# Causal corner of the transposed scores: set to zero by GpSimd after the exponential, in place of a mask product on PE before it

## The chip, the cores and the metric

One core of one Trainium2 chip runs the whole program. The metric is the device time in microseconds of one execution, and the time of a kernel is the median of its runs. The engines are PE (TensorE, matrix products into PSUM), DVE (VectorE), ACT (ScalarE), POOL (GpSimd) and SP (SyncE, which here only issues DMAs). Each engine works through its own instructions in order, and semaphores tie the engines together.

## The reference, cut to what matters

The program computes two transformer layers over 2 batches of 1024 tokens with 128 channels. The change touches the attention of layer 0:

```
Q, K, V = split_heads(h @ WQ.T), split_heads(h @ WK.T), split_heads(h @ WV.T)   # 16 heads of 8
scores  = einsum('bhqd,bhkd->bhqk', Q, K) / sqrt(8)
scores  = where(tril(ones(S, S)), scores, -1e9)
m       = max(scores, axis=-1)
e       = exp(scores - m)
out     = einsum('bhqk,bhkd->bhqd', e / sum(e), V)
```

After it come layer 0's mixture of 64 experts, a four-layer recurrent block (RWKV) and a mixture of 8 experts; none of them is edited. Attention wants an exact zero in e wherever the key comes after the query.

## The kernel before, in words

`build` runs `stage_front` (loads, layer norm, projections), `stage_core` (attention, then the 64 experts), `stage_rwkv_in`, `stage_rwkv` and `stage_last`. The 32 (batch, head) pairs are worked off in 8 groups of 4 heads (`NG`, `HG`).

In a group the scores are computed twice. **Fills** (`fills`, L693) compute them with queries on the partitions, up to 512 columns to a piece, into one of three PSUM banks; DVE takes the maximum of each piece (L1098), and PE may write a bank again only when the piece three items earlier has been reduced (`await_bank`). A group has 38 such pieces. The maxima are negated and split in three bf16 parts on DVE (`negate`, L1102), turned by PE (`turn_neg`, L748), copied by DVE to `neg_t` (L1128) and carried by three DMAs (L592) into three extra rows of `qa`. **Units** (`scores`, L713) then compute the transposed scores with keys on the partitions, the maxima already subtracted by those extra rows. A group has 24 units (`UNITS`: query chunk c of 512, key tile j of 128, pair p of heads): 8 with c=0 and 16 with c=1. A unit is two products of up to 512 columns, one per head. ACT takes the exponential of both (L945) into one of four slots of `pt`. Two units, p=0 and p=1, make one step q; after them `outputs` (L733) multiplies the four heads' `pt` with the values `va_g` into the accumulator bank: eight f32 products (L743).

A unit whose key tile lies on the diagonal (j >= 4c) gets, behind each of its two products, a third operand added into the first 128 columns of the bank: identity times `mask_kq` (L729), a 128x128 bf16 tile with -1e30 where the key comes after the query. There are 16 such units to a group, 4 in each step q, so 32 mask products a group and 256 in all. The fills have mask products of their own (L709, `mask_qk`), which are not edited.

PE's order is written out in `group` (L835): for each unit u the fills of `FRONT[u]`, perhaps a `turn_neg`, `scores(g, u)`, the fills of `BACK[u]`, and at odd u >= 3 `outputs` of step (u-3)/2, that is of the two units before last. The last step of a group is output after unit 1 of the next group; in the last group it follows at once. `SPREAD` deals the fills of group g+1 over the units of group g; group 0 does the rest of its own as well. The last group has no fills; beside its units run the output projection, layer norm, logits and routing of the first token chunks (`beside`). A unit waits for the exponential of the unit two before it (`prob_done`), ACT waits before it overwrites a slot of `pt` until the slot's `outputs` are done (`pv_done`).

POOL makes `ident`, `mask_qk`, `mask_kq` and zeroed `va_g` at the start (L191 to L206), and in attention it only copies the values of each group into one of the two `va_g` (`keep_v`, L679), when the outputs of the group two before have ended. SP's queue for each group: load of the group three ahead, then `pack` (results out of `acc`), then `neg_rows`.

Of the kernel before, what the change touches and what calls it, by code (L numbers as in the profile page):

```python
# [6 lines left out]
ALU = mybir.AluOpType  # L7
ACT = mybir.ActivationFunctionType
F32 = mybir.dt.float32
BF16 = mybir.dt.bfloat16  # L10
AX_X = mybir.AxisListType.X

P = 128
# [9 lines left out]
NG = B * H // HG  # L23
NEG = -1e30
# [36 lines left out]
def chunk(c, n=CH):  # L61
    return slice(c * n, (c + 1) * n)
# [54 lines left out]
def stage_front(nc, G, A):  # L117

    mem = G.mem
    with ExitStack() as ctx:  # L120
# [17 lines left out]
        pool_zero, const_done = mem.sem("pool_zero"), mem.sem("const_done")  # L138
# [15 lines left out]
        with nc.Block() as block:  # L154
# [34 lines left out]
            @block.gpsimd  # L189
            def _(pool):  # L190
                pool.memset(G.ident[:, :], 0.0).then_inc(pool_zero, 1)  # L191
                pool.memset(G.mask_qk[:, :], 0.0).then_inc(pool_zero, 1)
                pool.memset(G.mask_kq[:, :], 0.0).then_inc(pool_zero, 1)
                pool.wait_ge(pool_zero, 3)
                pool.affine_select(out=G.ident[:, :], in_=G.ident[:, :], compare_op=ALU.not_equal, fill=1.0, base=0,
                                   pattern=[[-1, P]], channel_multiplier=1).then_inc(const_done, 1)

                pool.affine_select(out=G.mask_qk[:, :], in_=G.mask_qk[:, :], compare_op=ALU.is_ge, fill=NEG, base=0,
                                   pattern=[[-1, P]], channel_multiplier=1).then_inc(const_done, 1)
                pool.affine_select(out=G.mask_kq[:, :], in_=G.mask_kq[:, :], compare_op=ALU.is_ge, fill=NEG, base=0,  # L200
                                   pattern=[[1, P]], channel_multiplier=-1).then_inc(const_done, 1)
                for k in range(2):
                    pool.memset(G.va_g[k][:, :, :, :], 0.0).then_inc(pool_zero, 1)
                pool.wait_ge(pool_zero, 5)
                for k in range(2):
                    pool.memset(G.va_g[k][:, :, :, 1:32:4], 1.0).then_inc(G.v_pad, 1)  # L206

# [47 lines left out]
            def _(dve):  # L255
# [44 lines left out]

                dve.memset(G.mean[:, :], 1.0 / P).then_inc(centre_done, 1)
                dve.memset(G.eps[:, :], 1e-5).then_inc(centre_done, 1)
                dve.wait_ge(const_done, 3)
                dve.tensor_scalar(G.centre[:, :], G.ident[:, :], -1.0 / P, None, ALU.add).then_inc(centre_done, 1)
                dve.tensor_copy(G.identb[:, :], G.ident[:, :]).then_inc(centre_done, 1)
                dve.memset(ones_row[:, :, :], 1.0).then_inc(centre_done, 1)
# [26 lines left out]
            def _(pe):  # L333
                def turn_x(c):
                    pe.wait_ge(x_in[c], 16)
                    if c == 3:
                        pe.wait_ge(x_kept, 2)
                    for t in range(4):
                        mm = pe.transpose(x_bank[c][:, chunk(t, P)], x_tok[:, 4 * c + t, :], G.ident[:, :])
                    mm.then_inc(x_turned, 1)  # L340
# [28 lines left out]
                        pe.wait_ge(x_kept, c)  # L369
                    ln_centre(pe, G, c, G.x[:, chunk(c)])  # L370

                pe.wait_ge(const_done, 3)
                turn_x(0)
                pe.wait_ge(centre_done, 4)
                centre(0)
# [3 lines left out]
                for i in range(3):  # L379
                    mm = pe.transpose(G.bank[4][:, chunk(i, P)], w_nat[:, i, :], G.ident[:, :])  # L380
# [63 lines left out]
def stage_core(nc, G, A):  # L444
# [4 lines left out]
    mem = G.mem  # L449
# [4 lines left out]
             for n in [min(HG, CH // min(CH, (i + 1) * P - k0))] for h in range(0, HG, n)]  # L454
    NF = len(FILLS)
    HALF = sum(i < 4 for _, _, i, _, _, _ in FILLS)

    UNITS = [(c, j, p) for c in range(2) for j in range(4 * c + 4) for p in range(2)]
    NU = len(UNITS)
    NQ = NU // 2  # L460
# [23 lines left out]
    LAST = NG - 1  # L484
# [9 lines left out]
    with ExitStack() as ctx:  # L494
# [3 lines left out]
        pt = m.sb("pt", [P, 4, 2, CH])  # L498
# [24 lines left out]
        hid = m.sb("moe_hid", [P, NC, CH])  # L523
        factor = [t[:, k, :, :].rearrange("p h t -> p (h t)").bitcast(F32) for t in (qa, ka) for k in range(2)]

        v_in = mem.sem("v_in")
        piece_psum, piece_max = mem.sem("piece_psum"), mem.sem("piece_max")
        max_step = mem.sem("max_step")
        neg_turned, neg_kept = mem.sem("neg_turned"), mem.sem("neg_kept")
# [1 line left out]
        score_psum, prob_done, pv_done = mem.sem("score_psum"), mem.sem("prob_done"), mem.sem("pv_done")  # L531
# [52 lines left out]
        with nc.Block() as block:  # L584
# [92 lines left out]
            @block.gpsimd  # L677
            def _(pool):
                def keep_v(k, g):  # L679
                    pool.tensor_copy(va_g[k][:, :, :, 0:32:4],  # L680
                                     G.va[:, bass.ds(g, 1), :, :].rearrange("p o t (h d) -> p (o t) h d", h=HG))\
                        .then_inc(v_in, 1)

                pool.wait_ge(G.v_pad, 2)
                for g in range(2):
                    keep_v(g, g)
                for g in range(2, NG):
                    pool.wait_ge(pv_done, NQ * (g - 1))
                    keep_v(g % 2, g)

            @block.tensor
            def _(pe):
# [20 lines left out]
                def scores(g, u):  # L713
                    c, j, p = UNITS[u]
                    q0 = max(CH * c, P * j)
                    n = CH * (c + 1) - q0
                    if u == 0:
                        pe.wait_ge(neg_in, 48 * (g + 2) if g else 48)
                    if NU * g + u == TURN_AT[0]:
                        pe.wait_ge(neg_in, 96)  # L720
                    if NU * g + u >= 2:
                        pe.wait_ge(prob_done, NU * g + u - 1)
                    for k in range(2):
                        out = score_bank[u % 2][:, k, :]
                        diagonal = j >= 4 * c
                        mm = pe.matmul(out[:, 0:n], ka[0:ROWS + 3, g % RING, 2 * p + k, chunk(j, P)],  # L726
                                       qa[0:ROWS + 3, g % RING, 2 * p + k, q0:q0 + n], start=True, stop=True)
                        if diagonal:
                            mm = pe.matmul(out[:, 0:P], G.identb[:, :], G.mask_kq[:, :], start=False, stop=True,  # L729
                                           skip_group_check=True)  # L730
                    mm.then_inc(score_psum, 1)

                def outputs(g, k, q):  # L733
                    c, j, _ = UNITS[2 * q]
                    q0 = max(CH * c, P * j)
                    n = CH * (c + 1) - q0
                    pe.wait_ge(prob_done, NU * g + 2 * q + 2)
                    if q == 0:
                        pe.wait_ge(v_in, g + 1)
                    if j == 0 and (not isinstance(g, int) or 2 * g + c):  # L740
                        pe.wait_ge(acc_kept, 2 * g + c)
                    for h in range(HG):
                        mm = pe.matmul(acc_bank[32 * h:32 * h + 32, q0 - CH * c:CH], va_g[k][:, j, h, :],  # L743
                                       pt[:, 2 * (q % 2) + h // 2, h % 2, 0:n], start=(j == 0),
                                       stop=(j >= 4 * c), skip_group_check=True)
                    mm.then_inc(pv_done, 1)
# [1389 lines left out]
def build(nc, A, out):  # L2136
    G = Global()
    with ExitStack() as ctx:
        mem = G.mem = Memory(nc, ctx)
# [3 lines left out]
        G.ident = mem.sb("ident", [P, P])  # L2143
        G.identb = mem.sb("identb", [P, P], BF16)
        G.mask_qk = mem.sb("mask_qk", [P, P], BF16)
        G.mask_kq = mem.sb("mask_kq", [P, P], BF16)
        G.mean = mem.sb("mean", [P, P])
        G.centre = mem.sb("centre", [P, P])
        G.eps = mem.sb("eps", [P, 1])
# [64 lines left out]
```

## Time and profile before

| | us |
|---|---|
| median of 3 runs | 1193.19 |
| runs | 1193.03 to 1208.87 |
| profiled execution | 1198.58 |
| its span, first to last instruction | 1196.7 |

| engine | busy in the span |
|---|---|
| PE | 1063.7 (89%) |
| DVE | 767.2 (64%) |
| ACT | 578.4 (48%) |
| POOL | 12.1 (1%) |

The profile is of one execution. The span covers first to last instruction; 1.9 us of the execution lie around it. PE's busy time has modelled ends, so a matmul's own duration is longer than the distance to the next one where they follow closely; for the cost of one in a row of them the distance between starts is read. PEclk is the granted clock of TensorE as a share of 2.4 GHz; it has two levels, 0.5 (1.2 GHz) and 1.

### The profile page before, as it was taken

How to read it: one execution, taken by the hardware profiler on the slowest of the kernel's cores; microseconds unless marked ns; L12 is line 12 of the kernel's file. 1: busy time of each engine (PE TensorE's matmuls, PEld its weight loads, DVE VectorE, ACT ScalarE, POOL GpSimd, SP SyncE). 2: the span in 40 equal slices, each digit the busy share in tenths (PEclk: the TensorE clock that was granted, in tenths of full speed). 3: DMA queues.
4: the chain of work that ended last, by engine and by line, in shares of the span. 5: the costliest groups of instructions: out<-in, count | busy, mean ns of one | idle time of the engine just before them, and what ended most of it. 6: DMA issues, size and time to landing. Idle time of an engine off the chain costs nothing. (4 is left out here: it accounts for less than half of the span.)

```text
span 1196.7 us, 13244 instructions
## 1 busy us (share of the span) xinstructions
PE 1063.7 (89%) x4046; PEld 463.8 (39%) x4046; DVE 767.2 (64%) x1327; ACT 578.4 (48%) x904; POOL 12.1 (1%) x26
## 2 busy tenths in 40 slices
PE   6788999999779999999999996498898898898698
PEld 3333444444334444444444432133333333343332
DVE  5867788887556555555555554676776776776465
ACT  5224566667644222222222224666666666767332
POOL 1000000000000000000000000000000000000000
PEclk9768999999989999999999999799899899899899
DMA  3721022200141545555555520000000000000100
GB/s 116 207 60 41 11 50 50 51 24 10 30 90 40 123 91 117 125 122 113 114 108 125 125 45 28 0 21 9 1 20 9 0 20 0 0 0 1 27 9 26
DMA packets 49975, 64.62 MB, mean 54 GB/s; under 512 B 17570, under 2 KB 41232, under 8 KB 45328
## 3 DMA queue, kind: packets, MB, share of 16 engines
q1 hardware_dynamic: 49100, 63.28, 22.5%
q10 hardware_dynamic: 832, 0.79, 0.2%
q8 instruction: 24, 0.39, 0.1%
q14 instruction: 19, 0.16, 0.0%
HBM read 55.87 MB, written 5.77 MB: 52 GB/s over the span
## 5 line engine op out<-in xcount | busy, mean ns | idle before, releaser
L1098 DVE TENSOR_REDUCE part_max<-psum 128x1 f32<-128x512 f32 (+3 forms) x304 | 188.1, 659 | 54.0 <-PE psum L709 31.6
L945 ACT ACTIVATE pt<-psum 128x1024 f32<-128x1024 f32 (+1 forms) x192 | 151.1, 813 | 141.1 <-PE psum L729 104.0
L1257 DVE TENSOR_TENSOR moe_gu<-moe_silu,psum 128x512 f32<-128x512 f32 x132 | 90.8, 688 | 152.0 <-PE psum L861 147.2
L1082 ACT ACTIVATE moe_silu<-psum 128x512 f32<-128x512 f32 x112 | 66.9, 597 | 200.0 <-PE psum L856 200.0
L856 PE MATMUL psum<-h,moe_wt 128*128 128x512 f32 x264 | 135.6, 595 | 1.6 <-ACT moe_silu L1050 1.6
L861 PE MATMUL psum<-h,moe_wt 128*128 128x512 f32 x264 | 135.2, 593 | 0.5 <-DVE moe_gu L1257 0.5
L866 PE MATMUL psum<-moe_hid,moe_wt 128*128 128x512 f32 x264 | 135.0, 593 | 0.7 <-DVE moe_hid L1265 0.7
L705 PE MATMUL psum<-ka,qa 72*128 72x512 bf16 (+3 forms) x384 | 121.8, 360 | 5.5 <-DMA ka<-rows_k 3.5
L726 PE MATMUL psum<-qa,ka 75*128 75x512 bf16 (+3 forms) x384 | 107.8, 344 | 7.1 <-DMA qa<-neg_t 6.8
L1265 DVE TENSOR_TENSOR moe_hid<-moe_gu,qa 128x512 f32<-128x512 f32 x120 | 83.1, 693 | 13.6 <-DVE moe_gu L1257 5.7
L1542 PE MATMUL psum<-kf,wt_c 128*128 128x512 f32 x128 | 67.8, 656 | 24.2 <-ACT kf L1671 24.2
L743 PE MATMUL psum<-pt,va_g 128*32 128x512 f32 (+3 forms) x768 | 86.6, 525 | 0.2 <-ACT pt L945 0.2
L861 PEld LDWEIGHTS psum<-h,moe_wt 128*128 128x128 f32 x264 | 49.9, 190 | 65.0 <-issue 61.5
L856 PEld LDWEIGHTS psum<-h,moe_wt 128*128 128x128 f32 x264 | 49.9, 191 | 64.3 <-issue 64.3
L1532 PE MATMUL psum<-mix_c,wt_c 128*128 128x512 f32 x128 | 62.9, 604 | 12.1 <-ACT relu L1668 12.1
L705 PEld LDWEIGHTS psum<-ka,qa 72*128 72x128 bf16 x384 | 39.3, 104 | 82.6 <-DVE part_max L1098 55.2
L866 PEld LDWEIGHTS psum<-moe_hid,moe_wt 128*128 128x128 f32 x264 | 48.0, 190 | 51.3 <-issue 49.5
L92 ACT ACTIVATE ln_sq<-psum 128x512 f32<-128x512 f32 x48 | 28.3, 602 | 57.3 <-PE psum L75 57.3
L83 PE MATMUL psum<-ln_sq,mean 128*128 128x512 f32 x96 | 50.1, 629 | 4.8 <-ACT ln_sq L92 4.7
L729 PE MATMUL psum<-mask_kq,identb 128*128 128x128 bf16 x256 | 53.5, 228 | 0.0
L726 PEld LDWEIGHTS psum<-qa,ka 75*128 75x128 bf16 x384 | 38.5, 103 | 38.3 <-DMA qa<-neg_t 8.4
L709 PE MATMUL psum<-mask_qk,identb 128*128 128x128 bf16 x256 | 53.3, 235 | 0.0
(251 smaller groups left out, 1394.7 us busy)
## 6 DMA issues: line engine op xcount, KB each, us to landing
qa<-comb_rows SPq DMA_DIRECT2D x56, 512.0 KB, 6.2
qa<-rows_q SPq DMA_DIRECT2D x21, 192.0 KB
ka<-rows_k SPq DMA_DIRECT2D x21, 192.0 KB
o_den<-acc SPq DMA_DIRECT2D x32, 64.0 KB, 2.2
moe_raw<-in_L_ffn_eg_w SPq DMA_DIRECT2D x32, 64.0 KB, 5.6
moe_raw<-in_L_ffn_eu_w SPq DMA_DIRECT2D x32, 64.0 KB, 5.4
moe_raw<-in_L_ffn_ed_w SPq DMA_DIRECT2D x32, 64.0 KB, 5.1
qa<-comb_rows SPq DMA_DIRECT2D x16, 128.0 KB, 3.1
```

Of the source, the lines that this page charges most:

```text
L705: mm = pe.matmul(bank[:, nk * h:nk * (h + 1)], qa[0:ROWS, g % RING, h0 + h, chunk(i, P)], ka[0:ROWS, g % RING, h0 + h, k0:k0 + nk], start= ...
L726: mm = pe.matmul(out[:, 0:n], ka[0:ROWS + 3, g % RING, 2 * p + k, chunk(j, P)], qa[0:ROWS + 3, g % RING, 2 * p + k, q0:q0 + n], start=True ...
L743: mm = pe.matmul(acc_bank[32 * h:32 * h + 32, q0 - CH * c:CH], va_g[k][:, j, h, :], pt[:, 2 * (q % 2) + h // 2, h % 2, 0:n], start=(j == 0 ...
L856: pe.matmul(g_bank[:, :], weights[:, 0, :], G.h[:, chunk(c)], start=True, stop=True).then_inc(g_psum, 1)
L861: pe.matmul(u_bank[:, :], weights[:, 1, :], G.h[:, chunk(c)], start=True, stop=True).then_inc(u_psum, 1)
L866: pe.matmul(y_bank[c][:, :], weights[:, 2, :], hid[:, at, :], start=first, stop=last, skip_group_check=True).then_inc(y_psum, 1)
L945: act.activation(pt[:, u % 4, :, 0:n], score_bank[u % 2][:, :, 0:n], ACT.Exp, scale=SCALE)\
L1082: act.activation(sg[:, c % 2, :], g_bank[:, :], ACT.Silu).then_inc(silu_done, 1)
L1098: dve.tensor_reduce(part_max[:, h0:h0 + heads, slot], bank_of("fill", f)[:, 0:heads * nk].rearrange("p (h n) -> p h n", h=heads), AX_X, AL ...
L1257: dve.tensor_tensor(gu[:, at % 2, :], sg[:, at % 2, :], u_bank[:, :], ALU.mult).then_inc(gu_done, 1)
L1265: dve.tensor_tensor(hid[:, at, :], gu[:, at % 2, :], tile[:, chunk(c)], ALU.mult).then_inc(hid_done, 1)
L1542: mm = pe.matmul(G.bank[4 + q][:, :], wt_c[:, WCV + j, :], kf[:, j, q, :], start=(j == 0), stop=(j == 3))
```

## The change

The 256 mask products and `mask_kq` go. POOL instead overwrites, after the exponential, the first 128 columns of both heads of a diagonal unit's slot of `pt` with zero where the key comes after the query: one `affine_select` of 128x256 f32 per diagonal unit, 16 a group, 128 in all. A diagonal step's `outputs` additionally waits for the two selects of its units (`masked`). `keep_v` for group g+1 now follows the eighth select of group g in POOL's queue.

```diff
-                pool.memset(G.mask_kq[:, :], 0.0).then_inc(pool_zero, 1)
-                pool.wait_ge(pool_zero, 3)
+                pool.wait_ge(pool_zero, 2)
...
-                pool.affine_select(out=G.mask_kq[:, :], in_=G.mask_kq[:, :], compare_op=ALU.is_ge, fill=NEG, base=0,
-                                   pattern=[[1, P]], channel_multiplier=-1).then_inc(const_done, 1)
...
-                dve.wait_ge(const_done, 3)
+                dve.wait_ge(const_done, 2)
...
-                pe.wait_ge(const_done, 3)
+                pe.wait_ge(const_done, 2)
...
+                def mask(g, u):
+
+                    pool.wait_ge(prob_done, NU * g + u + 1)
+                    pool.affine_select(out=pt[:, u % 4, :, 0:P], in_=pt[:, u % 4, :, 0:P], compare_op=ALU.is_ge, fill=0.0,
+                                       base=0, pattern=[[0, 2], [1, P]], channel_multiplier=-1).then_inc(masked, 1)
+
                 pool.wait_ge(G.v_pad, 2)
                 for g in range(2):
                     keep_v(g, g)
-                for g in range(2, NG):
-                    pool.wait_ge(pv_done, NQ * (g - 1))
-                    keep_v(g % 2, g)
+                for g in range(NG):
+                    for u in range(NU):
+                        c, j, _ = UNITS[u]
+                        if j >= 4 * c:
+                            mask(g, u)
+                        if u == 7 and 1 <= g < LAST:
+                            pool.wait_ge(pv_done, NQ * g)
+                            keep_v((g + 1) % 2, g + 1)
...
                     for k in range(2):
                         out = score_bank[u % 2][:, k, :]
-                        diagonal = j >= 4 * c
                         mm = pe.matmul(out[:, 0:n], ka[0:ROWS + 3, g % RING, 2 * p + k, chunk(j, P)],
                                        qa[0:ROWS + 3, g % RING, 2 * p + k, q0:q0 + n], start=True, stop=True)
-                        if diagonal:
-                            mm = pe.matmul(out[:, 0:P], G.identb[:, :], G.mask_kq[:, :], start=False, stop=True,
-                                           skip_group_check=True)
                     mm.then_inc(score_psum, 1)
...
                     pe.wait_ge(prob_done, NU * g + 2 * q + 2)
+                    if j >= 4 * c:
+                        pe.wait_ge(masked, 16 * g + 8 * c + 2 * (j - 4 * c) + 2)
```

## Rows read from the trace of the kernel before

**Rows 1.** The page: PE over the span, the clock in 40 slices, the mask products.

```profile
PE 1063.7 (89%) x4046; PEld 463.8 (39%) x4046; DVE 767.2 (64%) x1327; ACT 578.4 (48%) x904; POOL 12.1 (1%) x26
PEclk9768999999989999999999999799899899899899
L729 PE MATMUL psum<-mask_kq,identb 128*128 128x128 bf16 x256 | 53.5, 228 | 0.0
```

**Rows 2.** Windows: stretch, length, busy PE, PEld, DVE, ACT, POOL, clock, DMA.

```profile
115.00:120.00 5.00, 5.00 (x26) 2.20 (x25) 2.67 (x4) 2.70 (x4) 0.64 (x1) 0.51 0.62 133
182.24:212.47 30.23, 30.23 (x259) 13.96 (x258) 24.82 (x45) 19.42 (x27) 0.66 (x1) 1.00 0.22 50
212.47:214.72 2.25, 2.25 (x27) 1.48 (x26) 2.06 (x4) 2.25 (x5) 0.66 (x1) 1.00 0.75 160
217.16:219.41 2.25, 2.25 (x27) 1.35 (x26) 1.92 (x4) 0.87 (x2) 0.00 (x0) 1.00 0.40 73
240.20:242.70 2.50, 2.50 (x23) 1.10 (x21) 2.34 (x4) 1.11 (x2) 0.00 (x0) 1.00 0.35 99
```

**Rows 3.** Timeline of units 0 and 1 of group 4: start, duration, instruction.

```profile
211.59 1.94 ACT L945 ACTIVATE pt<-psum 128x1024 f32<-128x1024 f32 x2 [1.39 <-PE psum L729]
211.61 0.38 PE L726 MATMUL psum<-qa,ka 75*128 75x512 bf16 x1
211.82 0.22 PE L729 MATMUL psum<-mask_kq,identb 128*128 128x128 bf16 x1
211.88 0.38 PE L726 MATMUL psum<-qa,ka 75*128 75x512 bf16 x1
212.99 0.66 POOL L680 COPY va_g<-va 128x256 f32<-128x256 f32 x1 [29.57 <-PE psum L743]
214.72 1.07 PE L743 MATMUL psum<-pt,va_g 128*32 128x512 f32 x8
```

**Rows 4.** Timeline: a later step of the same group, and DVE's run of reduces.

```profile
209.06 5.55 DVE L1098 TENSOR_REDUCE part_max<-psum 128x1 f32<-128x512 f32 x8 [0.46 <-PE psum L709]
216.49 1.16 ACT L945 ACTIVATE pt<-psum 128x512 f32<-128x512 f32 x2 [1.07 <-PE psum L729]
219.41 0.64 PE L743 MATMUL psum<-pt,va_g 128*32 128x256 f32 x8
```

**Rows 5.** Timeline of group 0 at the low clock, its first and tenth mask, DVE behind.

```profile
55.63 0.31 PE L729 MATMUL psum<-mask_kq,identb 128*128 128x128 bf16 x1
66.67 0.31 PE L729 MATMUL psum<-mask_kq,identb 128*128 128x128 bf16 x1
66.78 0.53 PE L705 MATMUL psum<-ka,qa 72*128 72x384 bf16 x1
67.45 5.34 DVE L1098 TENSOR_REDUCE part_max<-psum 128x1 f32<-128x384 f32 x9 [0.47 <-PE psum L709]
```

**Rows 6.** Timeline: DMAs of the negated maxima, the wait at the end of group 0.

```profile
109.25 1.82 SPq L592 DMA_DIRECT2D qa<-neg_t  x3
114.53 0.39 PE L726 MATMUL psum<-qa,ka 75*128 75x512 bf16 x1 [2.77 <-DMA qa<-neg_t]
205.83 1.82 SPq L592 DMA_DIRECT2D qa<-neg_t  x3
```

**Rows 7.** Groups by line, POOL's selects.

```profile
L195 POOL TENSOR_SCALAR_AFFINE_SELECT ident<-ident 128x128 f32<-128x128 f32 x1 | 0.3, 294 | 0.2 <-POOL mask_kq L193 0.2
L1941 POOL TENSOR_SCALAR_AFFINE_SELECT expand<-expand 24x512 bf16<-24x512 bf16 x3 | 2.2, 746 | 0.4
```

**Rows 8.** Timeline: DVE beside a POOL memset at the start, and a larger one alone.

```profile
2.21 1.83 POOL L203 MEMSET va_g<- 128x1024 f32 x2
2.29 1.83 DVE L304 TENSOR_SCALAR centre<-ident 128x128 f32<-128x128 f32 x1 [1.27 <-POOL mask_kq L200]
308.32 0.49 DVE L1164 TENSOR_SCALAR h<-h,mod 128x512 f32<-128x512 f32 x1
```

**Rows 9.** Timeline: the end of the last group.

```profile
347.63 0.38 ACT L945 ACTIVATE pt<-psum 128x256 f32<-128x256 f32 x1
348.06 0.43 PE L743 MATMUL psum<-pt,va_g 128*32 128x128 f32 x8 [0.22 <-ACT pt L945]
```

More of the change, by code:

```diff
@@ L199, in _ @@
                                    pattern=[[-1, P]], channel_multiplier=1).then_inc(const_done, 1)
-                pool.affine_select(out=G.mask_kq[:, :], in_=G.mask_kq[:, :], compare_op=ALU.is_ge, fill=NEG, base=0,
-                                   pattern=[[1, P]], channel_multiplier=-1).then_inc(const_done, 1)
                 for k in range(2):
                     pool.memset(G.va_g[k][:, :, :, :], 0.0).then_inc(pool_zero, 1)
-                pool.wait_ge(pool_zero, 5)
+                pool.wait_ge(pool_zero, 4)
                 for k in range(2):
@@ L524, in stage_core @@
         factor = [t[:, k, :, :].rearrange("p h t -> p (h t)").bitcast(F32) for t in (qa, ka) for k in range(2)]
-        v_in = mem.sem("v_in")
+        v_in, masked = mem.sem("v_in"), mem.sem("masked")
         piece_psum, piece_max = mem.sem("piece_psum"), mem.sem("piece_max")
@@ L2145, in build @@
         G.mask_qk = mem.sb("mask_qk", [P, P], BF16)
-        G.mask_kq = mem.sb("mask_kq", [P, P], BF16)
         G.mean = mem.sb("mean", [P, P])
```

## The prediction

> **What bounds the kernel now.** I read the page first: PE is busy 89% of the span, and the clock row is 8 or 9 nearly throughout [rows 1]. That is an average, so the windows come next. One group of attention in its steady state is 30.23 us long, PE is busy for all of it, DVE for 24.82, ACT for 19.42 and POOL for 0.66, at the full clock (2.4 GHz) [rows 2]. Groups 2 to 5 all repeat this length: POOL's copy of the values, once a group, sits idle 29.57 us and works 0.66 [rows 3]. PE's busy time is modelled, so I checked it by distances in the timeline: a product of 512 columns takes 0.21 us to the next start, a mask product of 128 columns 0.06 [rows 3]. Products, outputs and masks follow one another like this through the whole group with no hole. So in this stage PE is the bound, and what leaves PE's stream shortens the group, until DVE (24.8) or something new takes over. Everything after attention (from about 350 us on) is untouched, and simply starts earlier.
>
> **Price of what goes.** There are 256 mask products [rows 1], 32 to a group. The mean of 228 ns on the page is latency, not cost. At the full clock one costs the 0.06 us from its start to the next product; I use 0.058, from the runs of such masks in the trace, of which [rows 3] has one. So 32 x 0.058 = 1.85 us per group at most. At the low clock (1.2 GHz) it is 66.78 - 66.67 = 0.11 us [rows 5]. Their weight loads run beside other products and are worth nothing.
>
> *Group 0.* Ten masks lie between 55.63 and 66.67, at the low clock, ahead of the point where DVE falls behind and runs nine reduces without a gap from 67.45 [rows 5]. They are on the path: 10 x 0.107 = 1.1 us. The rest of the group I cost at nothing, for two covers: up to about 108 us its units carry a whole group's fills in a dozen units, and DVE reduces without gaps; and from 109.25 to 114.53 the group's end waits for the negated maxima, PE idle for 2.77 us [rows 6]. PE only arrives there 0.5 us sooner and waits longer.
>
> *Group 1.* Eight masks at the low clock (the clock is 0.51 from 115 to 120 [rows 2]) and 24 at the full one: 0.86 + 1.39 = 2.2 us. I take off 0.1: 2.1.
>
> *Groups 2 to 6.* 1.85 each, less two things. First, DVE. In the steps from 240.20 to 242.70 (last of a group) and 212.47 to 214.72 (first of a group) DVE is busy 2.34 of 2.50 and 2.06 of 2.25 [rows 2]. With four masks (0.23) out of each, PE would want 2.27 and 2.02, 4.29 together, against 4.40 of DVE. The others have room (1.92 against 2.02 from 217.16 [rows 2]). Three banks smooth some of it; I take 0.25 us a group as lost to DVE, between 0.1 (the bare difference) and 0.6. Second, the new wait, below: 0.1. That leaves 1.5 a group; group 6 has a tail without fills, where PE already waits for ACT, so 1.2 there. 4 x 1.5 + 1.2 = 7.2 us.
>
> *Group 7.* PE waits here for DVE and ACT in the layer norm and routing chains, and some half of the 32 masks lie on the path: 16 x 0.06 = 1.0 us. Against it, the last step's outputs start 0.05 us after the last exponential (348.01 to 348.06) [rows 9]; now a select stands between, +0.65, and the packing of the last results hangs on it. Net +0.4 us, between -1.5 and +2.2.
>
> **Price of what comes.** A select of 128x256 f32 is not in the trace. Below, one of 128x128 f32 took 0.294; above, one of 512 elements a partition took 0.746 [rows 7]. On the line between them 256 elements make 0.294 + 128/384 x 0.452 = 0.44, and I take that, since the cost is nearest to a matter of elements a partition; a POOL copy of the same 128x256 took 0.66 [rows 3]. POOL's work is then 16 x 0.44 + 0.66 = 7.7 us of a group's 28.7: no bound. Around the select lie two releases. POOL's copy starts 0.09 us after the outputs' modelled end (212.90 to 212.99), and I allow 0.1 for the way back to PE: 0.65 us from the end of an exponential to the outputs, between 0.5 and 1.0.
>
> What is the room? The outputs of a step come two units after its own. The tightest step is the first of a group: exponentials end at 211.59 + 1.94 = 213.53, outputs start at 214.72, room 1.19 us [rows 3]. Without the eight masks of units 0 to 3 PE gets there 0.46 sooner, and the exponentials only 0.12 sooner: room 0.85. 0.65 fits, barely, and with 1.0 it costs 0.15; hence 0.1. The other diagonal steps have 1.7 us or more (217.65 to 219.41 [rows 4]), about 1.3 after the change. Behind a late `outputs` on PE stand the next fills and units, and on ACT the slot of `pt`; both are late by the same 0.1 and no more. The extra wait instruction on PE is free: the first step of a group has three waits and no larger gap than the others.
>
> DMAs: the maxima of the next group are issued from 205.83 to 207.65 [rows 6] and land some 1.9 later, near 209.6, and are wanted near 211: after the change still over 1 us early. `keep_v` now stands behind the eighth select, half a group ahead of its use: free. At the start a memset and a select of 128x128 go, 0.4 us of POOL, but PE's first transposes wait for the token DMA: nothing.
>
> **Lock on the SBUF port.** At the start a DVE operation of 128x128 took 1.83 us beside a POOL memset, where a 128x512 one in the last group took 0.49 [rows 8]. So the two engines can hold each other up. DVE's reduces from PSUM show none of it: eight in 5.55 us, 0.69 each, with POOL's copy of 0.66 among them [rows 3, 4]. The Trainium skill ("SBUF — State Buffer", section "SBUF: two separate sides") says that DVE and GpSimd share a port pair under an exclusive lock, which a DVE instruction takes when it has two SBUF inputs or runs in a 2-port mode. By that rule the reduces stay free, but the five small operations of `negate`, which fall among diagonal units, and the selects would stall each other.
>
> **Sum.** 1.1 + 2.1 + 7.2 + 0.4 = 10.8 us off the profiled 1198.58: 1187.8. The profiled execution is 5.4 above the median of the runs, 1193.19; against the median it is 1182.4, and I say 1182.
>
> **Rivals.**
> - *DVE takes over* (14%). For it: DVE is at 82% of a group and at 94% in its tightest step [rows 2]. If each handshake costs and a group gives 0.9 instead of 1.5, the gain is 7.5: about 1186. Against it: DVE still waits for PE in most steps.
> - *The lock* (12%). Up to three selects of 0.44 fall into the chain of negated maxima, whose transpose PE reaches 0.7 us after DVE is done. Delays of 0.9 to 1.3 would stop PE for some 0.4 a group; with seven groups, 2.8 us less: 1185. It decides where the delay passes 0.5 us. For it: [rows 8]; against: DVE's operations there are 0.18 us each.
> - *POOL becomes the bound, slower than before* (6%). In each half of a group eight selects must fit into about 8 us, from the first exponential's end to the fourth outputs. Beyond 1.0 us a select every tenth costs 0.8 us per half: 16 x (d - 1.0) a group. The gain is gone at d = 1.1; at d = 1.4 it is 8 x 6.4 = 51 us lost against 11 gained, 1233. Against it: no select took over 0.75 [rows 7].
> - *The clock* (8%). After idle stretches it stays low for some 10 us, as behind 114.53 [rows 2, 6]. PE idles a little longer there now and reaches the next units at other moments; half the clock for 5 us more or less is 2.5 us of PE. 1178 or 1186.
> - *Nothing is gained* (4%): the removed products were filler under a wait that the trace doesn't show. 1193.
>
> **Chances and range.** The forecast, 1179 to 1185, has 56%. If all 256 masks were earned, (238 x 0.058 + 18 x 0.107) = 15.7, it would be 1177.5; with clock luck 1175. The other side reaches to no gain and a little noise of the median: 1195. A measurement of this kernel tells about 2% (24 us) from no change. Faster by more is out of the masks' reach, 3% for the clock; slower by more needs POOL as bound, 5%; within, 92%.
>
> **What would show it.** Group periods near 28.7 at POOL's copies; no L729; selects near 0.44, and POOL's busy near 70 us; outputs' waits for POOL only in a group's first step and at the very end; DVE's busy per group unchanged at 24.8. Wrong would be: selects over 1 us, PE idle before L743 in many steps, or a group still of 30 us.

## The result and the profile after

| | before | after |
|---|---|---|
| median of 6 runs each, same chip (us) | 1199.82 | 1184.85 |
| lowest to highest | 1193.03 to 1208.87 | 1181.74 to 1187.65 |
| profiled execution / its span | 1198.58 / 1196.7 | 1187.65 / 1185.9 |

The ratio is 0.9878, with a 95% interval of 0.9829 to 0.9926: 1.2% faster, less than the 2% that the prediction named as tellable, but the interval leaves out 1. Two later repetitions of the changed kernel gave 0.992 [0.989, 0.9951] and 0.9863 [0.9817, 0.991]; a repetition of the kernel before gave 1.0018 [0.998, 1.0056]. Predicted was 1182 in a range of 1175 to 1195.

The page of the changed kernel, answering to [rows 1]: busy time of each engine, the clock in 40 slices, then the groups of the outputs and of the selects (busy, mean ns | idle before, and its releaser).

```profile
PE 1054.5 (89%) x3790; PEld 449.3 (38%) x3790; DVE 765.4 (65%) x1327; ACT 577.6 (49%) x904; POOL 63.7 (5%) x152
PEclk9769999999789999999999999799999999999799
L749 PE MATMUL psum<-pt,va_g 128*32 128x512 f32 (+3 forms) x768 | 86.3, 523 | 0.9 <-POOL pt L684 0.8
L684 POOL TENSOR_SCALAR_AFFINE_SELECT pt<-pt 128x256 f32<-128x256 f32 x128 | 52.4, 410 | 234.0 <-ACT pt L951 233.2
```

The 256 mask products are gone from PE's count (4046 to 3790). The selects took 52.4 us of POOL, and in the whole program PE waited 0.8 us for them. POOL itself mostly waits for ACT (233.2 us): it is nowhere near a bound.

Where did the time go? I laid the executions side by side by one landmark, ACT's first exponential of each group, and for the end PE's first product of the experts. The second pair is a later repetition of both kernels. "Gain" is before less after, in us; the spans' difference is the sum.

| stretch | predicted | before | after | gain | gain, second pair |
|---|---|---|---|---|---|
| start to group 0 | 0 | 56.52 | 60.73 | -4.2 | +2.9 |
| group 0 | 1.1 | 58.77 | 54.78 | +4.0 | +0.5 |
| group 1 | 2.1 | 35.84 | 29.67 | +6.2 | +5.9 |
| groups 2 to 5 | 6.0 | 120.91 | 114.96 | +6.0 | +5.9 |
| group 6 | 1.2 | 30.24 | 29.16 | +1.1 | +1.1 |
| group 7 | 0.4 | 46.14 | 48.01 | -1.9 | -2.2 |
| the rest | 0 | 848.28 | 848.59 | -0.3 | +0.3 |
| sum | 10.8 | 1196.7 | 1185.9 | 10.8 | 14.4 |

The sum of the first pair equals the predicted 10.8, and that is partly luck: groups 2 to 6 came as predicted, group 1 gave three times its term, the last group lost, and the start and group 0 vary from execution to execution.

A steady group answers to the second row of [rows 2]. The windows (stretch, length, busy PE, PEld, DVE, ACT, POOL, clock) of group 4 after the change:

```profile
202.82:231.48 28.66, 28.63 (x226) 11.81 (x225) 24.16 (x44) 19.34 (x26) 7.07 (x17) 1.00 0.23 54
```

28.66 us in place of 30.23, 33 fewer products counted, PE still busy all of it, POOL at 7.07 (predicted 7.7). PE is still the bound of this stage.

Because single executions differ by more than 10 us, here are all timed executions of this study, where each kernel's time stands against the mean granted clock of its core. At each of the ten clock levels that both have, the changed kernel is below the kernel before; five of them (means of the executions):

| mean granted clock | before: mean us (executions) | changed: mean us (executions) |
|---|---|---|
| 0.941 | 1208.5 (1) | 1190.7 (2) |
| 0.947 | 1198.2 (5) | 1187.1 (5) |
| 0.948 | 1194.9 (1) | 1186.2 (5) |
| 0.951 | 1194.1 (8) | 1182.6 (3) |
| 0.954 | 1192.0 (5) | 1181.5 (1) |

Ten of the 91 executions of the kernel before were in a slower state, over 1.5% above its fastest, and are left out of what follows. One straight line, common to all kernels, has 7.9 us for every 0.01 of clock, and the changed kernel lies 12.9 +- 1.0 us below the kernel before (81 and 24 executions). Their medians differ by 12.3, 1198.99 to 1186.68. So most of the spread of a kernel's times goes with the clock, and the gain is real and a little larger than the predicted 10.8.

### The profile page after: what moved, and what is told of

Same layout as the page of the kernel before. It is cut to its first block and busy times, and to the rows that moved or that the text cites. A ratio compares the mean times of both kernels' runs of the same rounds, so it can differ in the third digit from the quotient of the medians.

```text
span 1185.9 us, 12921 instructions
## 1 busy us (share of the span) xinstructions
PE 1054.5 (89%) x3790; PEld 449.3 (38%) x3790; DVE 765.4 (65%) x1327; ACT 577.6 (49%) x904; POOL 63.7 (5%) x152
## 5 line engine op out<-in xcount | busy, mean ns | idle before, releaser
L1104 DVE TENSOR_REDUCE part_max<-psum 128x1 f32<-128x512 f32 (+3 forms) x304 | 185.0, 658 | 39.7 <-PE psum L717 25.3
L733 PE MATMUL psum<-qa,ka 75*128 75x512 bf16 (+3 forms) x384 | 99.0, 343 | 5.2 <-DMA qa<-neg_t 4.9
L1548 PE MATMUL psum<-kf,wt_c 128*128 128x512 f32 x128 | 71.3, 686 | 24.2 <-ACT kf L1677 24.2
L684 POOL TENSOR_SCALAR_AFFINE_SELECT pt<-pt 128x256 f32<-128x256 f32 x128 | 52.4, 410 | 234.0 <-ACT pt L951 233.2
L1518 PE MATMUL psum<-hp,wt_a 128*128 128x512 f32 x96 | 50.0, 603 | 3.1 <-DVE hp L1755 3.1
```

The costliest lines, as they stand in the source:

```text
L1104: dve.tensor_reduce(part_max[:, h0:h0 + heads, slot], bank_of("fill", f)[:, 0:heads * nk].rearrange("p (h n) -> p h n", h=heads), AX_X, AL ...
L1548: mm = pe.matmul(G.bank[4 + q][:, :], wt_c[:, WCV + j, :], kf[:, j, q, :], start=(j == 0), stop=(j == 3))
```

## Experiments

All times are medians, and ratios are to the kernel before on the same chip.

### The two kernels again: r_before, r_after, r_after_again

No edit; they give the second traces.

> The kernel before, unchanged, for a second trace. Question: which parts of the gap between the two first traces belong to the change, and which to the execution. In the first traces the changed kernel's first exponential came 4.2 us later (60.73 against 56.52), its group 0 was 4.0 us shorter (54.8 against 58.8) and its group 1 was 6.2 us shorter (29.7 against 35.8), since no stretch at 1.2 GHz stood behind the wait for the maxima at the end of group 0. Theory 'luck': front, group 0 and group 1 of this kernel differ from its own first trace by several us, with the place of the slow-clock stretches, while groups 2 to 5 are again 30.23 us each. Theory 'structure': it repeats 56.5, 58.8 and 35.8 within 0.5 us.

> The changed kernel, unchanged. Both theories: groups 2 to 5 again 28.66 us (one or two 0.3 longer). 'Structure': group 1 again 29.7 us, since PE idles 0.84 us before it; 'luck': group 1 somewhere between 28.7 and 35. Total against the kernel before: 0.986 to 0.992 (the steady groups alone give 8 us, 0.7%).

> The changed kernel once more: last group 48.0, groups 2 to 5 28.66 to 29.0, group 1 29.66 us. Group 0 between 54.8 and 60.3 us, by the length of the slow-clock stretch (55 and 57 us so far).

Measured: r_before 1200.81 us; r_after 1187.05 us; r_after_again 1186.32 us. Their steady groups are 30.23 and 28.66 to within 0.01, as in the first traces, but for one (group 3 of r_after, 29.04, of which more below). Their group 0 is 57.36 before and 56.82 and 57.58 after (first traces 58.77 and 54.78): the same program differs there by 2.8 us between executions, so the 1.1 us predicted for this group can't be confirmed or refuted. The third trace of the changed kernel brought the largest surprise, a last group of 45.58 us instead of 48.01; it is taken up below.

### What do the selects cost? e_nomask

```diff
-                        if j >= 4 * c:
-                            mask(g, u)
...
-                    if j >= 4 * c:
-                        pe.wait_ge(masked, 16 * g + 8 * c + 2 * (j - 4 * c) + 2)
```

> The changed kernel without the 128 selects and without PE's waits for them; the upper corner of the diagonal tiles is left unmasked. It measures what GpSimd's part costs. My theory (hidden in the steady groups, 0.63 us at the last step and some port contention in the last group): groups 2 to 5 stay at 28.66 us, the last group (first exponential to the first expert product) is 1 to 2 us shorter than the 48.0 of the changed kernel, total 1 to 2 us faster. Rival (the select's latency or the port lock costs in every group): groups 2 to 5 fall to 28.4 us or below, since 32 mask products at 0.058 us are 1.85 us and only 1.57 were seen.

Measured: 1185.01 us, ratio 0.9891 [0.9858, 0.9924]. Group 4 of this kernel, same columns:

```profile
201.00:229.53 28.53, 28.53 (x226) 11.80 (x225) 24.26 (x45) 19.35 (x27) 0.65 (x1) 1.00 0.20 49
```

28.53 against 28.66: sixteen selects and the waits for them cost PE 0.13 us of a group. That is the price of the handshake in the steady state; predicted was 0.1. The profile shows no wait of PE for a select in these groups, so at which instructions the 0.13 arises stays open.

### Is DVE next? e_dve_half

The reduces read half of their columns; everything else is the changed kernel.

```diff
-    bank_of("fill", f)[:, 0:heads * nk].rearrange("p (h n) -> p h n", h=heads),
+    bank_of("fill", f)[:, 0:heads * nk].rearrange("p (h n) -> p h n", h=heads)[:, :, 0:nk // 2],
```

> The changed kernel, with DVE's maxima taken over the first half of each piece's columns alone (wrong maxima, DVE's work in attention about halved). The steady groups lost 30.23 - 28.66 = 1.57 us where 32 mask products at 0.058 are 1.85. Theory (the missing 0.28 us is DVE's, 0.13 of it seen without selects): groups 2 to 5 at 28.4 to 28.55 us. Rival (it is PE's own: the products cost less than 0.058 in place, or the selects' waits take it): 28.66 as before. Group 0, where DVE reduces without gaps for 12 us, gets 1 to 3 us shorter in either case.

Measured: 1185.75 us (2 runs), ratio 0.9883 [0.9802, 0.9965]. Its group 4:

```profile
201.82:230.24 28.42, 28.42 (x227) 11.82 (x225) 16.21 (x45) 19.35 (x26) 7.08 (x17) 1.00 0.25 60
```

With DVE at 16.21 instead of 24.5 a group takes 28.42. So DVE's work holds PE up by 0.24 us a group in the changed kernel, where 0.25 was predicted. If nothing else held PE up on either side, 30.23 - 28.42 = 1.81 us is what the 32 masks were worth, against 1.85 from the distances in the trace. The 0.24 here and the 0.13 of e_nomask can't be added: together they are 0.37, and a group came out only 0.28 above 30.23 - 1.85. Taking away either the selects or half of DVE's work removes a part of the same wait, and no run removes both.

### How much slower may the selects be? e_sel2 and e_sel3

The select is done two or three times in a row, each waiting for the one before (here three):

```diff
-                    pool.affine_select(...).then_inc(masked, 1)
+                    for i in range(3):
+                        ins = pool.affine_select(...)
+                        if i < 2:
+                            ins.then_inc(again, 1)
+                            again_n[0] += 1
+                            pool.wait_ge(again, again_n[0])
+                    ins.then_inc(masked, 1)
```

> The changed kernel with each select run twice. In the run with three, 34 selects stood in a row at 0.44 us from one to the next, so a unit cost 1.31 us and a diagonal step 2.62, and the steps' distance was 2.62: periods of 32.06. Theory (a step takes the longer of PE's own 2.0 to 2.9 us and twice the select): with 2 x 0.44 = 0.88 a unit, 1.76 a step, POOL stays below PE in every step; only the first step of a group, with 0.85 us of room, waits: periods 28.8 to 29.3 us. Rival (the latency of each select adds to every step): 8 x 0.44 = 3.5 us more, 32 us again.

> The changed kernel, with each select run three times in a row, each waiting for the one before (about 3 x 0.41 + 2 x 0.25 = 1.7 us per unit in place of 0.41). It looks for the point from which POOL decides. My rule in the prediction was 16 x (d - 1.0) us a group beyond d = 1.0: 16 x 0.7 = 11 us a group, periods near 40 us and the kernel some 80 us slower than the changed one. Rival (the room behind a step absorbs it: the steps' own period of 2.0 to 2.9 us holds two selects only up to about 1.1): the same sign, but counted as 2 x d against the step, 8 steps x (3.4 - 2.4) = 8 us a group, periods near 36.5 us.

Measured: e_sel2 1191.32 us, 0.993 [0.9887, 0.9973]; e_sel3 1208.51 us, 1.0072 [1.0033, 1.0111]. Windows of a steady group of each (e_sel2, then e_sel3):

```profile
176.70:205.80 29.10, 28.73 (x227) 11.79 (x226) 24.73 (x45) 19.34 (x26) 13.44 (x34) 1.00 0.23 53
```

```profile
184.39:216.45 32.06, 28.99 (x230) 12.08 (x225) 24.85 (x45) 19.42 (x27) 19.62 (x50) 1.00 0.20 47
```

The expectation for e_sel3 took each repeated select to be dearer than it is. In the trace they follow one another at 0.44 us (a run of them, below, with 19 in 8.25 us), so three make 1.31 us a unit, not 1.7, and both numbers expected for the group were too long.

```profile
184.04 8.25 POOL L685 TENSOR_SCALAR_AFFINE_SELECT pt<-pt 128x256 f32<-128x256 f32 x19
```

What happens is simple all the same. A diagonal step has two units, so 2 x 1.31 = 2.62 us of POOL, where PE alone needs 2.0 to 2.9; the outputs in this stretch come 2.6 to 2.7 us apart, and the group grows by 3.4 us. At 0.87 us a unit (e_sel2) only 0.4 is lost. The point from which POOL bounds a diagonal half thus lies between 0.87 and 1.31 us a unit; my rule 16 x (d - 1.0) gives 5.0 at 1.31 where 3.4 was measured. At three times the POOL work the kernel is 0.7% slower than before, at twice it is still 0.7% faster. For e_sel2 the expected period of 28.8 to 29.3 us came true (29.06).

### Masks back on PE in the last group, or in its last step: e_last_pe, e_last_pe_again, e_step_pe

```diff
-                        if j >= 4 * c:
+                        if j >= 4 * c and g < LAST:
                             mask(g, u)
...
+                        if g == LAST and j >= 4 * c:
+                            mm = pe.matmul(out[:, 0:P], G.identb[:, :], G.mask_kq[:, :], start=False, stop=True,
+                                           skip_group_check=True)
...
-                    if j >= 4 * c:
+                    if j >= 4 * c and g < LAST:
                         pe.wait_ge(masked, 16 * g + 8 * c + 2 * (j - 4 * c) + 2)
```

`mask_kq` is made again, as before the change. e_step_pe does the same for the last diagonal step only.

> The changed kernel, with the last group alone masked by PE as before (32 mask products at that place, no selects and no waits there). Theory (in the last group the products were mostly hidden and the select's latency is on the path at the end): last group 46 to 47.5 us against 48.0, total 0.5 to 2 us faster than the changed kernel, so the best version so far. Rival (the 1.9 us that the last group lost were a slow-clock stretch at another place): last group as long as in the changed kernel or longer by up to 1 us for the products.

> The changed kernel with the last group masked by PE, once more, beside the changed kernel. By the traces it should be 2.3 us (0.2%) faster, since the last group takes 45.7 us in place of 48.0. In its first run it was 0.5 us faster in the median, with an interval of 0.3%. Expected: 1 to 3 us under the changed kernel in the median, last group 45.5 to 46 us; group 0 anywhere from 54.8 to 60.3 us, with the length of the slow-clock stretch.

> The changed kernel, with the very last step (group 7, j = 7) alone masked by PE: 4 mask products back, 2 selects and their wait gone. The last group took 48.0 us with selects, 46.2 with no mask at all and 45.7 with products. Theory 'end': PE's wait of 0.77 us for the last select is on the path and is all that this step costs: 47.2 us; the remaining 1.3 us come from selects in front of DVE's work on layer norm and routing and from the earlier waits. Rival 'all of it': 46.2 us or less. Total 0.5 to 1 us under the changed kernel, within its noise.

Measured: e_last_pe 1186.59 us, 0.9912 [0.9878, 0.9946]; e_last_pe_again 1188.06 us, 0.9892 [0.9846, 0.9939]; e_step_pe 1187.44 us, 0.9881 [0.9821, 0.9941].

First the end itself. The timeline of the changed kernel's last units: the last exponential, the last select, the last outputs, the first product of the experts.

```profile
335.95 0.38 ACT L951 ACTIVATE pt<-psum 128x256 f32<-128x256 f32 x1
336.40 0.41 POOL L684 TENSOR_SCALAR_AFFINE_SELECT pt<-pt 128x256 f32<-128x256 f32 x1 [0.34 <-ACT pt L951]
336.96 0.42 PE L749 MATMUL psum<-pt,va_g 128*32 128x128 f32 x8 [0.77 <-POOL pt L684]
337.31 0.30 PEld L862 LDWEIGHTS psum<-h,moe_wt 128*128 128x128 f32 x2 [0.20 <-issue]
```

The exponential ends at 336.33, the outputs start at 336.96: 0.63 us with a select between, where [rows 9] had 0.05. The predicted chain was 0.65. With the masks back on PE (e_last_pe_again) it is 0.05 again:

```profile
331.49 0.38 ACT L957 ACTIVATE pt<-psum 128x256 f32<-128x256 f32 x1
331.92 0.43 PE L755 MATMUL psum<-pt,va_g 128*32 128x128 f32 x8 [0.42 <-ACT pt L957]
```

So 0.58 us at the end of the last group are the select's, shown. The rest of its 1.9 us are not. At first I put all of it down to the selects, because the last group was 48.01, 48.01 and 47.63 with selects (after, r_after, e_step_pe), and 45.69 and 45.05 without (e_last_pe twice), 46.16 in e_nomask. Then r_after_again, a repetition of the changed kernel, took 45.58 with all sixteen selects. The windows of the same stretch, 22 us after the group's first exponential, tell the two apart; the last three columns are clock, DMA share and GB/s. First the first trace of the changed kernel, then r_after_again:

```profile
311.30:321.30 10.00, 9.54 (x33) 3.61 (x32) 6.61 (x22) 5.23 (x8) 0.00 (x0) 0.53 0.13 33
```

```profile
311.82:321.82 10.00, 9.10 (x44) 3.44 (x44) 7.93 (x34) 6.73 (x10) 0.00 (x0) 0.83 0.12 32
```

The profile has 33 products of PE in one and 44 in the other. At 0.53 it spent almost the whole window at 1.2 GHz, at 0.83 a third of it. Both executions slowed down after the same stretch in which PE waited for other engines (the 6 us before it had PE busy 4.52); they differ in how soon the full clock came back. So the 2.4 us between these two executions of one kernel are a matter of the clock, not of selects in PE's way. They are in part paid back behind the group: "the rest" takes 851.67 us in r_after_again, against 848.63 in r_after. Over the first 20 products of PE behind the group it has the clock at 0.72 and takes 12.16 us, where the first trace of the changed kernel has 0.84 and takes 10.68:

```profile
335.40:347.56 12.16, 8.93 (x20) 3.78 (x17) 7.79 (x37) 4.69 (x7) 0.00 (x0) 0.72 0.41 107
337.31:347.99 10.68, 7.44 (x20) 3.31 (x17) 7.40 (x36) 4.69 (x7) 0.00 (x0) 0.84 0.58 121
```

Neither expectation of the other two runs came true. e_last_pe_again was to be 1 to 3 us faster than the changed kernel: its trace has the shorter last group, but its median is 1.7 us above that of r_after_again. e_step_pe was to have a last group of 47.2 us, or 46.2 by the rival: its last outputs follow their exponential by 0.05 us again, but the group took 47.63, with the long slow stretch in it. Of the version with the masks kept on PE no gain was measured: 1187.16 us, against 1186.68 of the changed kernel (18 and 24 executions; 1 or 2 us would not be seen in these medians).

r_after_again also shows what the edit is worth in this group at a like clock (0.88 up to the last exponential, in the kernel before 0.89). Its last exponential starts 44.22 us after the group's first one (289.82), in the kernel before 347.63 - 302.28 = 45.35 [rows 9]; its last outputs are again 0.63 behind that exponential's end:

```profile
334.04 0.38 ACT L951 ACTIVATE pt<-psum 128x256 f32<-128x256 f32 x1
335.05 0.42 PE L749 MATMUL psum<-pt,va_g 128*32 128x128 f32 x8 [0.98 <-POOL pt L684]
```

That is 1.13 us less without the masks. Against two other traces with masks on PE and a clock of 0.89 it is 0.80 (r_before, 45.02) and 0.68 (e_last_pe, 44.90). So 0.7 to 1.1 us are won by the masks that went, where 1.0 was forecast, and 0.58 given back by the select.

Whether the selects make the long slow stretch likelier stays open. Four of the five traces with single selects and full reduces have it (after, r_after, e_step_pe and e_after_pad, 47.6 to 48.0 us). Of the six whose last group has none, only e_before_pad has it (from 20 to 32 us into the group; 46.01 us, because it was spared a later stretch near 43 us that the first trace of the kernel before has). So it is not tied to them alone. But the traces do not acquit the selects: from the last group's first exponential to the end of the program the same five take 896.5 to 897.3 us, r_after_again the most, and the same six 893.5 to 895.3. Beside it stands that the medians show no gain for the version with the masks kept on PE.

### What made group 1 so much shorter? e_before_pad and e_after_pad

Group 1 gained 6 us, and the masks can't be worth more than 2.2. The windows of its first 8 us, kernel before, then changed kernel:

```profile
115.29:123.29 8.00, 8.00 (x37) 2.80 (x35) 4.06 (x6) 4.25 (x5) 0.64 (x1) 0.50 0.40 92
```

```profile
115.51:123.51 8.00, 7.88 (x68) 3.50 (x70) 7.07 (x12) 5.87 (x9) 3.15 (x8) 1.00 0.69 150
```

Before, PE had the low clock from 115.3 to about 125.3 (10 us, and as long in r_before). After, it had none in this group. What stands ahead is the wait for the negated maxima at the end of group 0: 2.77 us at 114.53 before [rows 6], 2.71 in r_before, and after the change only this:

```profile
111.75 1.82 SPq L589 DMA_DIRECT2D qa<-neg_t  x3
114.87 0.61 PE L733 MATMUL psum<-qa,ka 75*128 75x512 bf16 x2 [0.84 <-DMA qa<-neg_t]
```

From the first issue to the product are 5.28 us before and 3.12 after, although SP's queue issues the same transfers at the same distances (the next group's loads start 1.9 us behind the first of the maxima in both). Only the third of the three transfers is late. From its issue to its landing it took 4.0 us before and 1.8 after; the first two took 1.8 to 1.9 in both. The rows of the DMA view, for a window of 0.1 us inside the third's issue (before, after):

```profile
qa<-neg_t SPq DMA_DIRECT2D x1, 8.0 KB, 4.0
qa<-neg_t SPq DMA_DIRECT2D x1, 8.0 KB, 1.8
```

What is different is a transfer that no line of the kernel issues: one of PE's instruction fetches, the queue "q8 instruction" of the DMA view (packets, MB, share of 16 engines); that it is PE's is inferred from its place, which moves with PE's instruction count. In the kernel before it falls between 112.0 and 112.5, inside the wait; in the changed one, which has fewer PE instructions ahead of this place, it falls between 119.0 and 119.5, behind it.

```profile
q8 instruction: 1, 0.02, 11.8%
```

```profile
q8 instruction: 1, 0.02, 12.0%
```

To test that, I moved the fetch without touching the work. The edit is the same in both kernels, and puts 112 waits that are satisfied at once ahead of group 0 (56 PE instructions by my count, which no trace shows):

```diff
+                for _ in range(112):
+                    pe.wait_ge(G.v_pad, 2)
```

> The kernel before, with 56 more semaphore instructions on PE at the start of attention, on a semaphore long reached. Nothing else moves: only where PE's instruction fetches (one of 16 KB, 256 instructions, every 15 us or so) fall in the program. Reason: in both traces of the kernel before, a fetch stands at 112.25 and 113.0, inside the burst of group loads, 2.3 us before PE goes on, and PE's wait at the end of group 0 is 2.8 us; in the traces without mask products the fetch comes at 116 to 119 and the wait is 0.84. Theory 'fetch': the wait falls to about 0.8 us, no slow-clock stretch follows, group 1 goes from 35.5 to about 31.3 us and group 0 loses 2 us; total 5 to 7 us (0.5%) faster than the kernel before. Rival 'work' (the shorter group 1 comes from the mask products themselves, or from the maxima's DMA landing later): group 1 stays at 35.5 us and the wait at 2.8.

> The changed kernel with the same 56 instructions, which put the fetch back where the kernel before had it (32 mask products of two instructions each are gone before group 1, 8 waits have come). Theory 'fetch': the wait before group 1 is 2.5 to 3 us again, the clock falls behind it, group 1 takes 33 to 34.5 us against 29.7, and the total comes within 0.5% of the kernel before. Rival 'work': group 1 stays at 29.7 us.

Measured: e_before_pad 1200.39 us, 1.0017 [0.9985, 1.0049]; e_after_pad 1194.56 us, 0.9967 [0.993, 1.0005]. The same two rows of e_before_pad, where the fetch fell at 115.0 to 115.5, ahead of the transfers, and of e_after_pad, where it fell at 124.0 to 124.5, between issue and landing:

```profile
115.40 1.82 SPq L592 DMA_DIRECT2D qa<-neg_t  x3
118.53 0.39 PE L726 MATMUL psum<-qa,ka 75*128 75x512 bf16 x1 [0.63 <-DMA qa<-neg_t]
```

```profile
121.64 1.82 SPq L589 DMA_DIRECT2D qa<-neg_t  x3
126.26 0.60 PE L733 MATMUL psum<-qa,ka 75*128 75x512 bf16 x2 [2.34 <-DMA qa<-neg_t]
```

Together:

| kernel | fetch, us after the first issue | issue to product | PE's wait | clock, first 8 us of group 1 | group 1 |
|---|---|---|---|---|---|
| before | 3 | 5.28 | 2.77 | 0.50 | 35.84 |
| r_before | 3 | 5.21 | 2.71 | 0.50 | 35.53 |
| e_after_pad | 2.5 | 4.62 | 2.34 | 0.57 | 32.78 |
| after | 7 | 3.12 | 0.84 | 1.00 | 29.67 |
| e_before_pad | -0.4 | 3.13 | 0.63 | 1.00 | 31.11 |

The group came out a little under the 33 to 34.5 us expected for e_after_pad, and its total within the expected 0.5% of the kernel before. The third transfer took 1.9 us in e_before_pad and 3.3 in e_after_pad. The kernel with all its masks loses the long wait and the slow stretch when the fetch is moved out, and the changed kernel gets both when it is moved in. In every other trace of this study the product comes 3.12 us after the first issue, and no fetch falls within 7 us behind that issue. How the fetch holds the transfer up, no run shows. So the term "group 1" is 35.84 - 31.11 = 4.7 us of clock that follows the long wait, and 31.11 - 29.67 = 1.4 us of masks.

The totals seem not to follow. For e_before_pad 5 to 7 us of gain were expected, and nothing was measured. The traces show why: the added waits have a price of their own, ahead of group 0. PE's first fill stands 3.48 us idle in the kernel before and 8.94 in e_before_pad:

```profile
41.68 0.22 PE L705 MATMUL psum<-ka,qa 72*128 72x128 bf16 x1 [3.48 <-DMA ka<-rows_k]
48.82 0.26 PE L705 MATMUL psum<-ka,qa 72*128 72x128 bf16 x1 [8.94 <-DMA ka<-rows_k]
```

In e_after_pad it is 9.71, and in the twelve traces without added waits 3.2 to 3.9. So the waits cost 5 to 6 us. By the trace, e_before_pad wins 2.1 us at the end of group 0 (2.77 - 0.63) and 4.7 in group 1, and loses 5.5 to the waits. That leaves 1.3 us of gain, which its interval (from 0.9985) allows. e_after_pad's total can't be laid to the fetch alone either. It is 7.9 us above the changed kernel's, of which the waits are some 6. And its profiled execution, at 1201.73 one of the two slowest of ten, has a group 0 of 63.94 us, where the changed kernel's three traces have 54.8 to 57.6, with PE at the low clock for its first 48 us (0.50 from 62.97 to 110.9).

So some 6.6 us between the first two traces (1.9 of the wait and 4.7 of the clock) are owed to where the fetch fell, and not to the masks. That is about half of the total gain. A second estimate, from the totals, agrees in sign: with the waits in both kernels the fetch works against the changed kernel, and the change was worth 5.8 us (1200.39 to 1194.56) in place of 12.3.

## Why the prediction was right, and where it was not

- **A steady group**, forecast 28.7, measured 28.66. The parts hold: masks 1.85 (1.81), and against them 0.35 for DVE and the new wait (0.28 together; 0.24 and 0.13 taken singly, which overlap). The price by distances between starts was right; by the page's mean of 228 ns [rows 1] a group would have lost over 7 us.
- **The select**, 0.44 from the line between two others [rows 7], took 0.406, with 0.44 between starts in a row. Chain at the very end 0.65 (0.63). PE waited for a select once in the program, where I had also allowed for it in a group's first step: the room there, 0.85, was enough.
- **Group 1** is the term that was mis-sized: 2.1 forecast, 6.2 and 5.9 measured, of which only 1.4 are the masks'. I took both the 2.77 us wait and the slow clock behind it [rows 2, 6] as fixed and said that PE would wait longer. Both vanished, because the wait was long by accident of an instruction fetch. That the total still came out within the range is therefore partly luck: without the 6.6 us that hang on the fetch the gain would have been some 6 us, and the time near 1193, near the range's upper edge. The rival "the clock" named the place and expected PE to idle longer there; it idled less.
- **Group 0**: the wait alone gives 1.9 of its 4.0 in the first pair. The rest is within what executions of one kernel differ by.
- **Group 7**: forecast +0.4, measured -1.9 and -2.2. In the third trace it is +0.56 against the first of before (46.14 - 45.58), and the forecast's own parts hold there: masks 0.7 to 1.1 (1.0 forecast), select 0.58 (0.65). What was not foreseen is 2.4 us of slow clock in the other two, and that the third trace pays 3.0 us behind the group. Counted to the end of the program, no trace of the changed kernel gains anything from group 7 on.
- **Negated maxima**: "still over 1 us early" was wrong for group 3. There PE waited 0.15 us for them in the first trace and 0.21 in r_after, and the group is 28.99 and 29.04; in r_after_again it did not wait, and the group is 28.67.
- **The rivals.** DVE takes over: no, 0.24. Nothing gained: no. POOL as the bound: only at three times the selects' cost. The lock on the port: the place was there, the price was small. Where the last group's DVE operations fall beside selects, both stretch:

```profile
287.46 1.21 POOL L684 TENSOR_SCALAR_AFFINE_SELECT pt<-pt 128x256 f32<-128x256 f32 x2 [1.58 <-ACT pt L951]
287.56 0.85 DVE L1138 TENSOR_TENSOR o_den<-o_den,rden 128x512 f32<-128x512 f32 x1
295.16 0.95 POOL L684 TENSOR_SCALAR_AFFINE_SELECT pt<-pt 128x256 f32<-128x256 f32 x2 [1.53 <-ACT pt L951]
295.22 0.63 DVE L1170 TENSOR_SCALAR h<-h,mod 128x512 f32<-128x512 f32 x1
```

The shortest of these DVE operations take 0.68 and 0.49 us, here 0.85 and 0.63; the longest select took 0.856 where the median is 0.406. In the steady groups nothing of it is seen: DVE's time per group did not grow (24.82 before, 24.2 to 24.7 after). The Trainium skill ("SBUF — State Buffer", section "SBUF: two separate sides") says that a DVE instruction with two SBUF inputs or in a 2-port mode and a GpSimd instruction lock each other out of the port pair they share, whichever starts first. The trace agrees as far as it goes: reduces from PSUM are untouched, SBUF operations are not. Whether the `TENSOR_SCALAR` ran in such a mode, no trace shows. The price was 0.14 to 0.45 us an encounter, below the 0.5 from which the rival would have decided.

- **The base.** The median of three runs from which I subtracted, 1193.19, was low: over the 81 executions it is 1198.99. The time came out 2.9 above the forecast although more was gained than forecast. So in the time, too, two misses offset each other.
- **Two slips in the rivals' sums.** DVE's rival gives 10.8 - 5 x 0.6 = 7.8, not 7.5. And 2.5 us either way of 1182 are 1179.5 and 1184.5, not 1178 and 1186. Neither changes the range.

## What to carry to other kernels

Price a removed product by the distance to the next start in a gapless row, and only in stages where PE is the bound; there the sum came out within 0.1 us a group. Where PE's instruction count changed here, its instruction fetches behind that place moved too, and one that fell into a burst of transfers that PE waited for cost about as much as all the masks, by the wait and by the slow clock behind it. An edit that is meant to move only one thing has a price too: read it in the trace before judging by the total. Before explaining a difference of a few us in one stage, look at a second trace of the same program and at the granted clock of that stage.

## What the runs showed of the hardware

- An instruction fetch of PE (0.02 MB) inside a burst of loads went with 4.6 to 5.3 us from issue to use of the maxima, in place of 3.1; the third of the three transfers took 3.3 to 4.0 us to land, in place of 1.8 to 1.9.
- Behind the wait for the maxima of group 1, PE had the low clock for some 7 us (after 2.3 us of wait) and 10 us (after 2.7 and 2.8); after 0.6 to 0.8 us it kept 1.00. The same program had a stretch of about 10 us at 0.53 in the last group in two executions, and not in a third.
- 112 waits of PE on a semaphore already reached cost 5 to 6 us (8.94 and 9.71 us of idle time in place of 3.2 to 3.9).
- A difference of 0.01 in the mean granted clock went with 7.9 us of the program's 1190.
- `affine_select` in place on 128x256 f32 took 0.406 us, 0.44 from start to start in a dependent row.
